# A graph layer and a mixture of experts on one core: reordered gathers, row turns and statistics, and output banks filled by ScalarE

## What is computed

```python
x = x + relu(segment_sum(edge_w[:, None] * (layernorm(x) @ W)[src], dst, 1024) + bias)
xt = layernorm(x)                                      # 1024 x 512; 16384 edges above
scores = sigmoid(xt @ Wg.T + bg); w, idx = top_k(scores, 2); w = w / w.sum(-1)
nx = normalized xt
h  = silu(nx @ (gamma_e * W1_e) + b1'_e) * (nx @ (gamma_e * W3_e) + b3'_e)   # 64 experts, 512 -> 256
y  = sum over the two chosen experts of w * (h @ W2_e + b2_e)                # 256 -> 512
z  = (silu(nxs @ Ws1 + bs1) * (nxs @ Ws3 + bs3)) @ Ws2 + bs2                 # shared expert, width 32
x  = x + y + z
```

## Time and profile before

| | us |
|---|---|
| median of 3 runs (442.3 to 443.75) | 443.29 |
| the profiled execution | 443.8 |
| its span, first to last instruction | 442.0 |
| TensorE busy in the span | 401.3 |
| VectorE busy | 216.0 |
| GpSimd busy | 173.5 |
| ScalarE busy | 152.2 |

### The profile page before, as it was taken

One profiled execution on the slowest core, in us unless ns is written; L12 is line 12 of the kernel. 1 busy time (PEld: TensorE's weight loads), 2 busy tenths in 40 slices (PEclk: granted clock), 3 DMA queues, 4 the chain that ended last, 5 costly groups with the idle time before them and its releaser, 6 DMA issues.

```text
span 442.0 us, 6556 instructions
## 1 busy us (share of the span) xinstructions
PE 401.3 (91%) x1905; PEld 210.6 (48%) x1906; DVE 216.0 (49%) x703; ACT 152.2 (34%) x380; POOL 173.5 (39%) x275
## 2 busy tenths in 40 slices
PE   6789999999999988899999999997788789889865
...
GB/s 255 205 348 408 406 267 6 135 30 24 25 25 202 157 311 53 205 367 409 402 406 407 409 405 408 407 405 409 407 407 407 406 405 407 404 404 314 56 264 310
DMA packets 44022, 129.15 MB, mean 292 GB/s; under 512 B 8054, under 2 KB 9270, under 8 KB 43858
## 3 DMA queue, kind: packets, MB, share of 16 engines
...
## 4 chain that ended last, share of the span: by engine, by line
PE 80%; DVE 8%; issue 6%; DMA 3%; ACT 1%; SPq 0%; DVEq 0%; POOL 0%; ACTq 0%; POOLq 0%
PE bank L1463 27%; PE bank L1329 12%; PE bank L1493 12%; PE bank L1278 5%; PE bank L1485 5%; PE bank L1251 5%; PE bank L1454 4%; PE bank L1317 2%; DMA w<-totals 2%; PE bank L1350 1%; PE bank L1223 1%; PE bank L1338 1%; DVE stats L803 1%; PE bank L1477 1%; PE bank L1470 1%
## 5 line engine op out<-in xcount | busy, mean ns | idle before, releaser
L1120 DVE SCALAR_TENSOR_TENSOR osl<-bank,b13T,osl 128x64 f32<-128x64 f32 x128 | 27.6, 277 | 158.2 <-ACT osl L734 158.2
L1463 PE MATMUL bank<-w,xhT 128*64 128x512 f32 x352 | 83.8, 619 | 15.6 <-issue 13.6
L727 ACT COPY xh<-bank 128x512 f32<-128x512 f32 x33 | 19.4, 586 | 146.3 <-PE bank L1463 126.2
L1329 PE MATMUL bank<-HW,AT 128*128 128x512 f32 x128 | 58.2, 592 | 0.0
L1463 PEld LDWEIGHTS bank<-w,xhT 128*64 128x64 f32 x352 | 26.0, 141 | 58.6 <-issue 55.2
L591 POOL DMA_INDIRECT totals<-osl,A x16 | 16.2, 1015 | 84.2 <-PE bank L1454 69.8
L591 POOL DMA_INDIRECT totals<-GW,A x16 | 16.2, 1014 | 81.5 <-PE bank L1454 64.7
L1493 PE MATMUL bank<-w,osl 128*64 128x512 f32 x176 | 41.9, 594 | 0.6 <-DVE osl L1120 0.6
L587 POOL DMA_INDIRECT A<-nx_rows,A x33 | 34.2, 1036 | 12.2 <-issue 9.6
L1329 PEld LDWEIGHTS bank<-HW,AT 128*128 128x128 f32 x128 | 22.9, 191 | 21.0 <-issue 21.0
L734 ACT ACTIVATE osl<-bank,b13T 128x64 f32<-128x64 f32 x128 | 29.9, 315 | 5.2 <-remote 1.9
(11 more groups left out here) (240 smaller groups left out, 602.0 us busy)
## 6 DMA issues: line engine op xcount, KB each, us to landing
...
```

The source lines that it names most:

```text
L1120: ins = v.scalar_tensor_tensor(hT[b][:, m, CAP * h:CAP * h + CAP], bank[4][:, (HC + m) * P + CAP * h:(HC + m) * P + CAP * h + CAP], b13T[: ...
L1329: ins = t.matmul(bank[4 + s % 2][:, :], AT[:, s % 2, k, :], HW[:, k, :], start=(k == 0), stop=(k == NB - 1))
L1463: ins = t.matmul(bank[2 + b][CAP * h:CAP * h + CAP, :], xe[b][:, c, CAP * h:CAP * h + CAP], up_w[v][:, h, :, c, :], start=(c == 0), stop=( ...
```

## The change

- `BY_DVE` goes from 4 to 1: for blocks 1 to 7 ScalarE writes `back[i][:, 0]` times the share into the PSUM bank, and TensorE adds the placed rows onto it with `start=False`. `diag` and its eight matmuls and four VectorE operations go; VectorE's first multiply-add remains for block 0 only. Banks get another order, and three whole-bank matmuls (`whole_bank`) write full banks beforehand.
- ScalarE copies result 31 ahead of `hidden(32)`.
- Ten `keep_busy` transposes stand ahead of the down-projection of step 31 instead of eight behind it; seven and a whole-bank matmul stand in place of fourteen ahead of the last.
- GpSimd issues the first four gathers in a row, then `stacked(7)`.
- TensorE turns the rows of step 1 in the middle of the first up-projection, and those of step 2 right behind it.
- Statistics blocks: blocks 4 and 5 move from step 4 of the first pair to step 7, blocks 6 and 7 from step 6 of the first pair to step 4 of the second; GpSimd's inverse deviations follow. VectorE's pairs and GpSimd's second pair are written out instead of looped.
- TensorE loads the offsets of eight tiles at once instead of four.

```diff
--- before.py
+++ after.py
@@ -41,7 +41,7 @@
 YS = 4
 NOWHERE = 60000.0
 EX, LAST = PAIRS - 1, PAIRS
-BY_DVE = NB // 2
+BY_DVE = 1
 XS = EX % YS
 
 
@@ -204,7 +204,6 @@
 
         zero_tile = w13[:, RING - 1, 0, :, :].rearrange("p c h -> p (c h)")[:, 0:D]
         place_last = [w2[:, RING - 2 + i // 4, (i // 2) % 2, 256 * (i % 2):256 * (i % 2) + P] for i in range(NB)]
-        diag = {i: w2[:, RING - 2 + i // 4, (i // 2) % 2, 256 * (i % 2) + P:256 * (i % 2) + 2 * P] for i in range(BY_DVE, NB)}
         wsh, tokf, token_at = small[:, 240:241], small[:, 241:242], small[:, 244:252]
         share_at, at_block, at_rank = (small[:, i:i + 1].bitcast(i32) for i in (242, 243, 252))
 
@@ -230,7 +229,7 @@
         LATE = 5
         late_turn = [PAIRS - 12, PAIRS - 10, PAIRS - 8]
         rank_bank, list_bank = bank[2], bank[3]
-        last_bank = [bank[i] for i in (0, 1, 3, 5, 7, 2, 4, 6)]
+        last_bank = [bank[i] for i in (4, 1, 3, 5, 7, 0, 2, 6)]
         
 
 
@@ -296,7 +295,7 @@
         back_in = [sem(f"back_in{i}") for i in range(NB)]
         zero_ready, zero_out, share_out, share_at_ready, wsh_in = (sem(i) for i in (
             "zero_ready", "zero_out", "share_out", "share_at_ready", "wsh_in"))
-        last_places, last_ps, diag_ready = sem("last_places"), sem("last_ps"), sem("diag_ready")
+        last_places, last_ps, bank_filled = sem("last_places"), sem("last_ps"), sem("bank_filled")
         x_final = sem("x_final")
         out_done = sem("out_done")
         held = sem("held")
@@ -478,6 +477,8 @@
             inverse_deviations(range(1, 2), 2)
             pool.wait_ge(edges_ready, 1)
 
+            DEVIATIONS = {(0, 5): 2, (1, 0): 4, (1, 6): 6}
+
             def pair(r, j, first):
 
                 half = (r * (NB // 2) + j) * 4
@@ -488,8 +489,8 @@
                     g.tensor_copy(keyw[h % 2], eT[:, 0:3:2, ds(j * 32 + 8 * h, 8)]).then_inc(key_copied, 1)
                     pool.wait_ge(key_copied, half + (h + 1))
                     for q in (2 * h, 2 * h + 1):
-                        if first and q in (5, 7):
-                            b = q - 3
+                        if isinstance(j, int) and (j, q) in DEVIATIONS:
+                            b = DEVIATIONS[j, q]
                             inverse_deviations(range(b, b + 2), b // 2 + 2)
                         if not first or q >= 4:
                             pool.wait_ge(quad_done[q % 2], half + (q // 2 - 1))
@@ -501,8 +502,8 @@
                         ins.then_inc(m_pool, 1)
 
             pair(0, 0, True)
-            inverse_deviations(range(6, NB), 5)
-            with pool.Fori(1, NB // 2) as j:
+            pair(0, 1, False)
+            with pool.Fori(2, NB // 2) as j:
                 pair(0, j, False)
             R1 = pool.value_load(rounds_sb[0:1, 0:1], min_val=1, max_val=N // WIN)
             with pool.If(R1 > 1):
@@ -594,8 +595,7 @@
             pool.wait_ge(list_ready, 1)
             for j in range(AHEAD):
                 gather(TOK[:, j:j + 1], j)
-                if j == 0:
-                    stacked(NB - 1)
+            stacked(NB - 1)
             pool.wait_ge(list_in, 16)
             for s in range(DRAM_BLOCKS, NB):
                 scatter_records(s)
@@ -751,21 +751,24 @@
             for j in range(PAIRS + 1):
                 if j >= 2:
                     act.wait_ge(hT_ps, j - 1)
-                hidden(j, j % 2)
+                if j < LAST:
+                    hidden(j, j % 2)
                 if j:
                     if j - 1 >= YS:
                         act.wait_ge(y_out[(j - 1) % YS], 16 * ((j - 1) // YS))
                     result(j - 1, (j - 1) % 2, (j - 1) % YS)
+                if j == LAST:
+                    hidden(j, j % 2)
                 if j >= 2:
                     act.wait_ge(hT_ready, j - 1)
                 if j == EX:
                     act.wait_ge(tokens_ready, 1)
                     over_silu(j, j % 2, 0)
+                    R2 = act.value_load(rounds_sb[0:1, 1:2], min_val=1, max_val=OVER)
                 else:
                     silu(j, j % 2, lambda h: slice(2 * pair_of(j) + h, 2 * pair_of(j) + h + 1))
             act.wait_ge(y_out[LAST % YS], 16 * (LAST // YS))
             result(LAST, LAST % 2, LAST % YS)
-            R2 = act.value_load(rounds_sb[0:1, 1:2], min_val=1, max_val=OVER)
             with act.If(R2 > 1):
                 with act.Fori(1, R2) as t:
                     j = act.snap(t + PAIRS)
@@ -775,6 +778,12 @@
                     act.wait_ge(y_out[XS], t * 16 + 16 * (LAST // YS - 1))
                     hold(act)
                     result(j, 0, XS)
+            for i in range(BY_DVE, NB):
+                act.wait_ge(back_in[i], 16)
+                if i == NB - 1:
+                    act.wait_ge(y_ready, R2 + LAST)
+                    hold(act)
+                a.activation(last_bank[i][:, :], back[i][:, 0, :], ACT.Identity, scale=share[:, i, 1:2]).then_inc(bank_filled, 1)
 
         @block.vector
         def _(dve):
@@ -895,6 +904,8 @@
                 dve.wait_ge(quad_done[q % 2], done + (q // 2 + 1))
                 v.tensor_tensor(to, to, bank[q % 4][:, 0:QW], ALU.add).then_inc(a_chain, 1)
 
+            STATS = {(0, 3): range(2, 4), (0, 7): range(4, 6), (1, 4): range(6, NB)}
+
             def sum_pair(r, j, with_x, first, last=False):
 
                 for q in range(8):
@@ -914,22 +925,24 @@
                         sums(r, j - 1, q - BEHIND + 8)
                     if q % 2 == 0 and not (with_x and first and q < 4):
                         low_pair(j, q // 2)
-                    if with_x and first and q in (3, 4, 6):
-                        c = {3: 2, 4: 4, 6: 6}[q]
-                        mean_and_variance(range(c, c + 2))
+                    if with_x and (j, q) in STATS:
+                        mean_and_variance(STATS[j, q])
                     if with_x and first and q in (5, 6):
                         dve.wait_ge(rstd_ready, 3)
                         standard_rows(q - 3, q - 5)
                     if with_x and not first and not last and q % 4 == 1:
-                        dve.wait_ge(rstd_ready, 5)
+                        dve.wait_ge(rstd_ready, b // 2 + 3)
                         dve.wait_ge(xhT_ps, b + 1)
                         standard_rows(b + 2, u)
 
             def all_pairs(r, with_x):
                 sum_pair(r, 0, with_x, True)
-                with dve.Fori(1, NB // 2 - 1) as j:
-                    sum_pair(r, j, with_x, False)
-                sum_pair(r, NB // 2 - 1, with_x, False, True)
+                if with_x:
+                    for j in range(1, NB // 2):
+                        sum_pair(r, j, True, False, j == NB // 2 - 1)
+                else:
+                    with dve.Fori(1, NB // 2) as j:
+                        sum_pair(r, j, False, False)
                 for q in range(8 - BEHIND, 8):
                     sums(r, NB // 2 - 1, q)
 
@@ -1178,11 +1191,8 @@
                     ins.then_inc(last_places, 1)
                 else:
                     product(j, j % 2, lambda h: slice(2 * pair_of(j) + h, 2 * pair_of(j) + h + 1))
-                if j == EX - 1:
-                    for i in range(BY_DVE, NB):
-                        ins = v.tensor_scalar(diag[i], ident[:, :], share[:, i, 1:2], None, ALU.mult)
-                    ins.then_inc(diag_ready, 1)
-            R2 = dve.value_load(rounds_sb[0:1, 1:2], min_val=1, max_val=OVER)
+                if j == EX:
+                    R2 = dve.value_load(rounds_sb[0:1, 1:2], min_val=1, max_val=OVER)
             with dve.If(R2 > 1):
                 with dve.Fori(1, R2) as t:
                     j = dve.snap(t + PAIRS)
@@ -1265,17 +1275,17 @@
                         if not (last and u):
                             x_rows(j * 2 + u + 1, 1 - u)
                     for q in range(4 * u, 4 * u + 4):
-                        _, at = nc.values_load_multi_w_load_instructions(
-                            tile_at[0:1, ds(j * 32 + QUAD * q, QUAD)], engines=[mybir.EngineType.PE],
-                            min_val=0, max_val=QW - TW, skip_runtime_bounds_check_because="DVE bounded them by min, and a tile's window starts after its quad's")
                         if q % 2 == 0:
+                            _, at = nc.values_load_multi_w_load_instructions(
+                                tile_at[0:1, ds(j * 32 + QUAD * q, 2 * QUAD)], engines=[mybir.EngineType.PE],
+                                min_val=0, max_val=QW - TW, skip_runtime_bounds_check_because="DVE bounded them by min, and a tile's window starts after its quad's")
                             pe.wait_ge(osl_ready, half + (q // 2 + 1))
                             pe.wait_ge(osl_pair, half + (q // 2 + 1))
                         pe.wait_ge(m_pool, quad + (q + 1))
                         pe.wait_ge(m_ready, quad + (q + 1))
                         pe.wait_ge(zeroed, quad + (q + 1))
                         for k in range(QUAD):
```

(35 more changed lines are left out.)

## The result

| kernel | median, us (runs) | ratio to the kernel before, 95% interval | gain, us |
|---|---|---|---|
| before | 443.12 (442.3 to 443.75) | | |
| changed | 437.24 (435.6 to 438.14) | 0.9858 [0.9826, 0.989] | 5.9 |
| forecast | 433.0 (430.9 to 436.7) | | 10.3 |

The direction was right; 4.4 us of the gain didn't come. The profiled execution took 438.14 us with a span of 436.4 (before 443.8 and 442.0), so the two profiles differ by 5.6 us. They are compared stage by stage. The lines of code have moved: TensorE's up-projection is L1463 before and L1476 after, the read back L437 and L436.

What follows compares the result with a forecast made beforehand. Bounds: VectorE and TensorE in the first stage, the weight stream for the experts, a result-31-to-VectorE-adds chain at the end. Gains 0.5 + 2.8 + 7.0 = 10.3 us gave 433.0 us (chance 0.57), range 430.9 to 436.7.

Steps and rivals of the forecast that it cites:

- first stage: Sparse matrix build beside `x @ W`, to 77 us: moved statistics and straight loops gain 0.5 us, bounds -0.5 and +1.5.
- stream: Expert weights: an earlier second up-projection lets the second load follow the first without a gap; 2.8 us, bounds 1.9 and 3.6.
- end: End stage: earlier copy of result 31 and read-back, fewer VectorE operations; gain 7.0 us, bounds 3.5 and 7.8.
- the thin windows of rows 3: Weight DMA at 17 GB/s over 185 to 187 us and 78 over 187 to 189; filling them was worth 3.5 us.
- the stream gains nothing: Rival: the thin windows only move, as the second load's start-up is not hidden; 0 to -0.6, 436.2 us, chance 0.10.
- both large gains halved: Rival: read-back slower beside output writes and stream at its lower bound; 0.9 and 3.5 less, 437.4 us, chance 0.05.
- keep it as late: First stage, second pair: GpSimd's two small deviation operations, about 1 us a block, move with the statistics, leaving GpSimd as late.
- a clock that stays low in the end stage: Rival: ten transposes fail to hold the clock, so the end gives 3.7 us; time 436.3 us, chance 0.13.
- step (a): End stage: ten transposes before the over-expert's down-projection keep the clock up; its matmuls take 1.8 us instead of 3.5.
- Late code: Rival: unrolled pairs at 30 to 60 us wait twice for instruction fetches, 12.2 us; time 445.2 us, chance 0.05.
- contention: Expert start: `stacked(7)` on GpSimd may block VectorE's adds through shared SBUF access, making the gain up to 0.9 us smaller.
- the gain of 1.5 us that hung on it: Rival, first stage: straight-line code counts in full, 1.5 instead of 0.5, with the end at 7.8; 431.2 us, chance 0.10.

Runs made afterwards that it cites:

- e4: Kernel before with only the end-stage edits (ScalarE fills, result 31 ahead of hidden(32), transposes, whole-bank matmuls): 438.42 us, ratio 0.987.
- e9: Kernel before without the six record scatters of blocks 5 to 7: 440.2 us, ratio 0.9924.
- e13: Kernel before with the record scatters of blocks 5 to 7 moved one block each behind the fifth, sixth and seventh gather: 442.51 us, ratio 0.9954.
- e5: Kernel before, unchanged, a second profiled execution: 445.31 us.
- e3: Changed kernel without the six record scatters of blocks 5 to 7: 433.56 us, ratio 0.9762.
- e10: Changed kernel with the record scatters of blocks 5 to 7 moved one block each behind the fifth, sixth and seventh gather: 434.9 us, ratio 0.9795.
- e8: Changed kernel with GpSimd's inverse deviations of blocks 4 and 5 two quads later in the second pair: 435.57 us, ratio 0.9842.
- e2: Kernel before with only the early turns of the rows of steps 1 and 2: 444.28 us, ratio 1.001.
- e14: Kernel before with the record scatters spread behind the fifth to seventh gather and the early turns of steps 1 and 2: 442.06 us, ratio 0.9935.
- e7: Changed kernel with twelve unread transposes ahead of up-projection 30's wait for its weights: 436.4 us, ratio 0.9826.

## Why the prediction was wrong

The gain of the profiles, term by term: first stage 0.69 (forecast 0.5), stream 0.09 (forecast 2.8), clock of up-projection 30 -1.70 (in no term of the sum), end 6.56 (forecast 7.0). Together that is 5.64 instead of 10.3.

**Failed step: the stream's 2.8 us.** Between the first up-projection and up-projection 30 the changed kernel gains 0.09 us. Two inferences stood on the thin windows of rows 3. The first was that the late second up-projection (rows 4) made them. In that execution it did leave the stream without requests: the load was issued only at its end, and over 186 to 187 us the share is 0.00. But e4, e9 and e13 have the same code there, start it after 0.4 us and issue the load in time, and e4's stream takes as long as before (221.77 and 221.74 us). What held in two of the five profiles with that code (before and e5) was taken for a property, and the stream's length did not hang on it. The second was that a load issued earlier would flow earlier. It was issued 4 us earlier (182.49, before 186.60), and its packets were slow behind the record scatters; without these, or with them spread, they are not (e3, e9, e10). One cause hid another at the same place. The prediction had weighed "the stream gains nothing" at 0.10, for another reason than the one found; its 436.2 is 1.0 us from the measured 437.24. The nearest rival by number is "both large gains halved" with 437.4, but that is luck: it has a stream that gains 0.9 less and an end that gains half, and neither came. The record scatters stand in no step of the prediction, although they are issued beside the very load that it counted on.

**First stage: 0.5 forecast, 0.44 measured** at its end (the first transposes of A start at 77.79, before 78.23), 0.69 at the first up-projection. The size was right. The cause was only half right: VectorE was to set the second pair; GpSimd did, through a wait of 3.34 us where the prediction had two small operations that "keep it as late". The wait was worth another 1 us in e8's profile.

**End: 7.0 forecast, 6.56 measured** in the first two profiles, 6.7 in the mean of all, 5.8 by e4's ratio. By steps: the over-expert's four rows 1.96 us (1.8 forecast); the whole banks 1.88 (1.8); result 31's copy 5.69 earlier, which is 6.61 from the start of the stage, as that came 0.92 later (6.9 forecast); the read back issued 3.98 after the copy began (416.64 - 412.66), where copy 411.45 and first landing 418.6 were forecast. `product(32)` came at 420.42, which less the 0.92 is 419.50, within the forecast's 419.3 to 420.1. VectorE stood 0.48 and 0.60 for blocks 2 and 3, of which 0.4 was in the sum; that is the 0.7 us by which the end of the last add (433.67, less 0.92 it is 432.75) missed the forecast's 432.1. ScalarE's fill takes 0.69 us (bound 0.80 from rows 12). The seven fills were hidden behind VectorE, but not by much: the last one begins at 430.69, and VectorE's last four adds at 431.20.

**The clock.** The rival of a clock that stays low in the end stage did not come true. That the ten transposes held it is not shown, for the 3.5 us of rows 7 were a single event too. In e5, the kernel before again, TensorE's timeline has

```profile
411.77 1.96 PE L1477 MATMUL bank<-w,osl 128*128 128x512 f32 x4 [1.77 <-DVE osl L1130]
```

and so it is, 1.96 us after a pause of 1.76 to 1.77, in all five later profiles with the old end stage (e2, e5, e9, e13, e14). Their end stages, 41.9 to 43.7 us and 42.9 in the mean, are not clearly shorter than the first one's 43.0. So no run shows that the clock's part of step (a) was worth anything; the new order and the fills are what is left, and they were not tried apart from each other.

The clock also acted where nobody looked: up-projection 30, after 1.74 to 1.84 us of pause, ran at the lower clock in four of the profiles (changed kernel, e4, e5, e13: 5.35 us) and at the full one in ten, after 1.74 to 1.98 us. It is worth 1.7 us in an execution; e7 gives 1.3 at the median, with overlapping intervals.

**Late code and contention.** Straight-line code made no late fetch that shows, as the Trainium skill (Runtime: NRT & Kernel Launch, Instruction fetch mechanics) says of crossings between blocks of code, which it has mostly hidden: in the second and third pair the only pause that VectorE's timeline shows is 0.39 us at 59.59, for TensorE. But the gain of 1.5 us that hung on it did not come either: the third product moved by 0.11 us (46.89 to 46.78). The contention of VectorE and GpSimd (the Trainium skill, SBUF — State Buffer, Who interferes with whom) was at most small: VectorE's four half rows took 0.42 us each beside `stacked(7)`, as before; GpSimd's five operations took 0.1 us more in two cases (0.35 and 0.57 instead of 0.26 and 0.44).

**Range.** The 436.7 left out the case that one large term is zero and another a little small. Both large terms were read from one execution, and two of its rows, the second up-projection of rows 4 and the over-expert's 3.5 us of rows 7, were not how the kernel mostly runs; 0.57 for the full sum was too much.
